# Splitting eight product groups among the last attention's score units

## What is computed

```
x = x + layernorm(attention(layernorm(x)))     # 16 heads of 64, causal, two null keys
x = x + layernorm(experts(layernorm(x)))       # four experts, the best two of a token weighted
# experts:
e0 = (silu(x @ sw_w1) * (x @ sw_w3)) @ sw_w2
e1 = gelu(sym @ me_c1w + b) @ me_c2w
e2 = h2 @ ce_gen_w
e3 = gelu(x @ ml_w1 + b) @ ml_w2
out = sum over the chosen e of weight_e * e
```

## Time and profile before

| | |
|---|---|
| median of three runs | 927.98 us (927.37 to 929.27) |
| span of the profiled execution | 927.0 us |
| PE busy | 867.1 us (94%) |
| DVE busy | 765.1 us (83%) |
| ACT busy | 585.8 us (63%) |
| POOL busy | 562.4 us (61%) |

### The profile page before, as it was taken

One profiled execution on the slowest core, in us unless ns is written; L12 is line 12 of the kernel. 1 busy time (PEld: TensorE's weight loads), 2 busy tenths in 40 slices (PEclk: granted clock), 3 DMA queues, 4 the chain that ended last, 5 costly groups with the idle time before them and its releaser, 6 DMA issues.

```text
span 927.0 us, 21283 instructions
## 1 busy us (share of the span) xinstructions
PE 867.1 (94%) x8062; PEld 689.6 (74%) x8062; DVE 765.1 (83%) x2457; ACT 585.8 (63%) x1255; POOL 562.4 (61%) x503
## 2 busy tenths in 40 slices
PE   0898899999999999999999999999999999999886
PEld 0685678688777878788787878678787878778676
DVE  6787799889898899889998899888998688865577
ACT  4518773967658672966648673866838774786631
POOL 5227763586638764586746865487644864467723
PEclk9989999999999999999999999999999999999999
DMA  6400000000000000000000000000000000000000
GB/s 165 113 1 0 13 2 2 1 12 2 14 1 0 13 2 13 1 13 1 14 1 1 13 2 14 0 13 2 2 13 1 1 13 2 1 1 1 3 12 12
DMA packets 21991, 11.46 MB, mean 12 GB/s; under 512 B 7552, under 2 KB 21248, under 8 KB 21760
## 3 DMA queue, kind: packets, MB, share of 16 engines
q1 hardware_dynamic: 20032, 9.50, 3.7%
q10 hardware_dynamic: 1856, 0.59, 0.3%
HBM read 7.99 MB, written 2.10 MB: 11 GB/s over the span
## 4 chain that ended last, share of the span: by engine, by line
PE 68%; DVE 16%; ACT 11%; issue 3%; POOL 1%; DMA 0%; SPq 0%; DVEq 0%; ACTq 0%; POOLq 0%
PE bank L1771 9%; PE bank L1772 8%; PE bank L1773 8%; PE bank L1784 5%; PE bank L2029 5%; PE bank L2086 4%; PE bank L1937 4%; PE bank L2035 3%; PE bank L2212 2%; PE bank L2218 2%; PE bank L2101 2%; PE bank L2076 2%; PE bank L2088 2%; PE bank L2187 2%; PE bank L2079 1%
## 5 line engine op out<-in xcount | busy, mean ns | idle before, releaser
L938 POOL TENSOR_TENSOR rnorm<-sumsq,minus_half 128x16 f32<-128x16 f32 x32 | 93.9, 2946 | 55.2 <-DVE sumsq L1574 55.2
L2029 PE MATMUL bank<-qT,kT 64*128 64x256 f32 x512 | 97.3, 387 | 0.0
L944 POOL TENSOR_TENSOR rnorm<-unit,minus_half 128x16 f32<-128x16 f32 x32 | 93.9, 2939 | 4.2 <-DVE unit L1580 4.2
L2035 PE MATMUL bank<-qT,kT 64*128 64x128 f32 x512 | 84.0, 284 | 5.1 <-ACT unit L1208 2.7
L1202 ACT ACTIVATE square<-bank,bias_k,rnorm 128x256 f32<-128x256 f32 x128 | 65.6, 570 | 35.8 <-PE bank L2029 35.8
L2035 PEld LDWEIGHTS bank<-qT,kT 64*128 64x128 f32 x512 | 71.0, 186 | 18.7 <-issue 5.7
L952 POOL TENSOR_SCALAR_AFFINE_SELECT square<-square 128x512 f32<-128x512 f32 x64 | 45.0, 704 | 61.6 <-ACT square L1208 61.5
L1132 ACT ACTIVATE xaT_hi<-bank 128x256 fp32r<-128x256 f32 x16 | 5.9, 382 | 111.1 <-PE bank L1945 110.7
L2029 PEld LDWEIGHTS bank<-qT,kT 64*128 64x128 f32 x512 | 68.7, 186 | 0.2
L2101 PE MATMUL bank<-w_out,qT 128*128 128x128 f32 x512 | 62.8, 276 | 1.2 <-DVE qT L1623 1.2
L1202 ACT ACTIVATE unit<-bank,bias_k,rnorm 128x256 f32<-128x256 f32 x96 | 51.4, 574 | 17.5 <-PE bank L2029 17.5
(11 more groups left out here) (419 smaller groups left out, 2902.7 us busy)
## 6 DMA issues: line engine op xcount, KB each, us to landing
xin<-in_L_attn_x SPq DMA_DIRECT2D x7, 256.0 KB, 2.8
out<-x SPq DMA_DIRECT2D x7, 256.0 KB, 2.3
square<-in_L_attn_w_kv SPq DMA_DIRECT2D x1, 1024.0 KB, 6.5
unit<-in_L_attn_w_q SPq DMA_DIRECT2D x1, 512.0 KB, 5.1
w_out<-in_L_attn_w_out SPq DMA_DIRECT2D x8, 64.0 KB, 2.1
xin<-in_L_attn_x ACTq DMA_DIRECT2D x1, 256.0 KB, 3.1
unit<-in_L_ffn_experts_gate ACTq DMA_DIRECT2D x1, 256.0 KB, 3.4
unit<-in_L_ffn_experts_up SPq DMA_DIRECT2D x1, 256.0 KB, 2.9
```

The costliest lines, as they stand in the source:

```text
L938: pool.tensor_tensor(rnorm[:, 1, t, :], sumsq[:, t % 2, :], minus_half[:], ALU.pow).then_inc(a_root.sem, 1)
L944: pool.tensor_tensor(rnorm[:, 0, ts, hs], k_sumsq[:, ts, hs], minus_half[:, hs].unsqueeze(1).to_broadcast([P, 2, H // 2]), ALU.pow).then_i ...
L2029: return mm(bank[s][:, 2 * P * i:2 * P * (i + 1)], kT[rs, p, 2 * P * b:2 * P * b + P], qT[rs, p, 2 * P * b:2 * P * (b + 1)], start=True, s ...
L2035: return mm(bank[2][:, 2 * P * s + P * i:2 * P * s + P * (i + 1)], kT[rs, p, ts], qT[rs, p, ts], start=True, stop=True)
```

## The change

The tables of PE and DVE for `LAST_A` are rewritten; those of ACT and POOL stay as they are. In the rest of the code, the operands of the last but one group's `f_out` go to buffers that attention does not use, and its results go in turn to banks 5 and 6. Each `f_out` can be asked for in two parts: part 0 is the products of `sw` and `me`, part 1 those of `gen` and `ml`.

```diff
@@ LAST_A
     "PE": """
-a_t.3 f_ce2T f_ml.3 a_v.2 a_v.3 f_out.0 a_scores.0 f_out.1 f_out.2 f_out.3 a_scores.1 a_nT a_mix.0 a_scores.2
-a_mix.1 a_scores.3 a_mix.2 a_scores.4 a_mix.3 a_scores.5 a_mix.4 a_scores.6 a_mix.5 a_scores.7 a_mix.6 a_out.0
-a_mix.7 a_out.1 F_turn.0 F_ce.0
+a_t.3 f_ce2T f_ml.3 a_v.2 a_v.3 a_scores.0 f_out.0.0 f_out.0.1 a_nT a_scores.1 a_mix.0 f_out.1.0 a_scores.2
+a_mix.1 f_out.1.1 a_scores.3 a_mix.2 f_out.2.0 a_scores.4 a_mix.3 f_out.2.1 a_scores.5 a_mix.4 f_out.3.0 a_scores.6
+a_mix.5 f_out.3.1 a_scores.7 a_mix.6 a_out.0 a_mix.7 a_out.1 F_turn.0 F_ce.0
     "DVE": """
-f_hid.1 a_ss.2 a_u.1 a_u.2 f_hid.2 a_ss.3 f_ce2 f_hid.3 f_ce2_apply a_u.3 f_pick a_nexp f_out.0 a_kss f_out.1
-f_out.2 f_out.3 a_nT a_mix.0 a_mix.1 f_end_stats a_mix.2 a_mix.3 a_mix.4 a_mix.5 a_mix.6 f_end a_o.0 a_mix.7 a_end.0
+f_hid.1 a_ss.2 a_u.1 a_u.2 f_hid.2 a_ss.3 f_ce2 f_hid.3 f_ce2_apply a_u.3 f_pick a_nexp a_kss f_out.0 a_nT
+a_mix.0 a_mix.1 f_out.1 a_mix.2 a_mix.3 f_out.2 a_mix.4 a_mix.5 f_out.3 a_mix.6 f_end_stats f_end a_o.0 a_mix.7 a_end.0
@@ buffers
+        hid_sw_late = [conv[:, 0, :], conv[:, 3, :], x1[:].rearrange("p t d -> p (t d)"), xn[:].rearrange("p t d -> p (t d)")]
+        hid_ml_late = [decay_row[:], *(unit_flat[:, i * N:(i + 1) * N] for i in (2, 3, 4))]
...
         def mix_bank(g, t):
+            if beside_ending(g):
+                return bank[5 + t % 2]
@@ POOL, late sum of units 0 and 1
-                    pool.wait_ge(f_e.sem, f_e.at(g - 1))
+                    if not ending(g):
+                        pool.wait_ge(f_e.sem, f_e.at(g - 1))
@@ ACT, f_ml
-                if j == 0 and not (known(g) and g == G - 1):
+                if j == 0 and g < G - 2:
                     act.wait_ge(a_ss.sem, a_ss.at(g + 1))
@@ PE, a_mix.0
+                elif ending(g):
+                    pe.wait_ge(f_meg.sem, f_meg.at(g - 1))
+                    pe.wait_ge(f_relu.sem, f_relu.at(g - 1))
                 else:
                     pe.wait_ge(f_eb.sem, f_eb.at(g - 1))
@@ PE, a_out.0
-                    if not ending(g):
+                    if ending(g):
+                        pe.wait_ge(f_eb.sem, f_eb.at(g - 1))
+                    else:
@@ PE, f_out
-            def f_out(g, t):
+            def f_out(g, t, part=None):
...
+                if beside_ending(g) and t > 1 and part != 1:
+                    pe.wait_ge(f_eb.sem, f_eb.at(g, E1 * (t - 1)))
```

More of the change, by code:

```diff
@@ L658, in ml_bank, with beside_ending, hid_sw_at, hid_ml_at @@
             return bank[2 + j % 2] if ending(g) else bank[4 + j % 2]
+        def beside_ending(g):
+            return g == G - 2
+        def hid_sw_at(g, j):
+            return (hid_sw_late if beside_ending(g) else hid_sw)[j]
+        def hid_ml_at(g, j):
+            return (hid_ml_late if beside_ending(g) else hid_ml)[j]
         def mix_bank(g, t):
+            if beside_ending(g):
+                return bank[5 + t % 2]
             return bank[(4, 5, 0, 1)[t]] if ending(g) else bank[4 + t]
@@ L1230, in f_ml_ @@
                 act.wait_ge(f_ml.sem, f_ml.at(g, j + 1))
-                if j == 0 and not (known(g) and g == G - 1):
+                if j == 0 and g < G - 2:
                     act.wait_ge(a_ss.sem, a_ss.at(g + 1))
-                act.activation(hid_ml[j], ml_bank(g, j)[:], ACT.Gelu, bias=b_ml[:, j:j + 1]).then_inc(f_mlg.sem, 1)
+                act.activation(hid_ml_at(g, j), ml_bank(g, j)[:], ACT.Gelu, bias=b_ml[:, j:j + 1]).then_inc(f_mlg.sem, 1)
             def f_ce_apply(g):
@@ L1710, in f_sw @@
                 gate, up = sw_banks(g, j)
-                V.scalar_tensor_tensor(out=hid_sw[j], in0=tanh_f(g, j), scalar=1.0, in1=gate[:], op0=ALU.add, op1=ALU.mult).then_inc(s.sem, 1)
+                hid = hid_sw_at(g, j)
+                V.scalar_tensor_tensor(out=hid, in0=tanh_f(g, j), scalar=1.0, in1=gate[:], op0=ALU.add, op1=ALU.mult).then_inc(s.sem, 1)
                 dve.wait_ge(s.sem, s.at(g, 2 * j + 1))
-                V.tensor_tensor(hid_sw[j], hid_sw[j], up[:], ALU.mult).then_inc(s.sem, 1)
+                V.tensor_tensor(hid, hid, up[:], ALU.mult).then_inc(s.sem, 1)
             def f_out(g, t):
@@ L2199, in f_ce2_apply @@
                 turn(bank[6], lambda t: ce_rows[:, t, :]).then_inc(f_gT.sem, 1)
-            def f_out(g, t):
+            def f_out(g, t, part=None):
                 ts = slice(t * P, (t + 1) * P)
-                if t == 0:
+                if t == 0 and part != 1:
                     pe.wait_ge(f_mlg.sem, f_mlg.at(g))
                     pe.wait_ge(f_meg.sem, f_meg.at(g))
-                    if ending(g):
+                    if ending(g) or beside_ending(g):
                         pe.wait_ge(f_hid.sem, f_hid.at(g))
-                    else:
+                    if not ending(g):
                         pe.wait_ge(f_cec.sem, f_cec.at(g))
+                if beside_ending(g) and t > 1 and part != 1:
+                    pe.wait_ge(f_eb.sem, f_eb.at(g, E1 * (t - 1)))
                 out_b = mix_bank(g, t)
[L2211 to L2214, removed]
+                if part != 1:
+                    for j in range(J1):
+                        mm(out_b[:, 0:P], hid_sw_at(g, j)[:, ts], w_sw2[:, j, :], start=(j == 0), stop=(j == J1 - 1))
+                    for j in range(2):
+                        mm(out_b[:, P:2 * P], hid_me[j][:, ts], w_c2[:, j, :], start=(j == 0), stop=(j == 1))
+                if part == 0:
+                    return
                 if not ending(g):
@@ L2217, in f_out @@
                 for j in range(J1):
-                    done = mm(out_b[:, 3 * P:], hid_ml[j][:, ts], w_ml2[:, j, :], start=(j == 0), stop=(j == J1 - 1))
+                    done = mm(out_b[:, 3 * P:], hid_ml_at(g, j)[:, ts], w_ml2[:, j, :], start=(j == 0), stop=(j == J1 - 1))
                 done.then_inc(f_e.sem, 1)
```

## The result

The changed kernel takes 936.15 us, the median of four runs (932.17 to 938.06), against 928.47 us for the kernel before, timed beside it: a ratio of 1.008, interval 1.006 to 1.010. Measured again with more runs, it took 934.46 against 928.36 us, a ratio of 1.0067 [1.0054, 1.0079]. With two more profiled executions there are twelve, with a median of 934.3, some 5.8 us over the kernel before; the first four alone are 7.7 us over it. The forecast was 931.8 (+3.8) with a range up to 934.0: the sign was right, the size was not.

What follows compares the result with a forecast made beforehand. It took the loop as bound by the PE-ACT ring (4.55 us a unit) and the end by one chain with 0.1 us slack on DVE. Loop −0.3, end +2.6, clock +1.5 gave +3.8: 931.8 us, range 929.6 to 934.0.

Steps and rivals of the forecast that it cites:

- The clock: PE's stop at the loop's start halves its clock for some 3 us of work: +1.5 us, ends 0 and 2.7.
- rival 2: A second clock fall at PE's stops ahead of `a_mix.7` and `a_out.1`: +1.5 us more, 933.3 us; chance 0.15.
- The end: On DVE, statistics behind `a_mix.6` and the wait for POOL's root delay the steps queued behind: +2.6 us.
- The loop: From unit 1 to `a_mix.6`: earlier start, less the added pieces and 0.2 us for hand-overs, net −0.3 us.
- Its first half: At the loop's start, unit 1 begins on PE at about 844.4, 1.3 us earlier.
- The pieces: Six `f_out` parts among the units, 7.4 us into some 5 us of waits: +0.8 us, ends 0 and +1.3.
- The turn: In a 4.55 us turn PE has 3.6 us taken, 0.94 free; pieces of 1.34 or 1.12 overrun by 0.4 or 0.2.
- The turn of 5.38 us: Unit 4's turn, with more exponentials on ACT: the added piece is free there.
- Rival 3: Not slower, the 2.6 us tail is hidden behind an earlier `a_mix.6`: about 926.4 us, or 927.9; chance 0.10.
- Rival 1: No clock fall at the loop's start: +2.3 us, 930.3 us; chance 0.15.
- Rival 4: Loop loses more: pieces +1.3, clock fall at its upper end 2.7; +5.5 us, 933.5 us or more; chance 0.13.

Runs made afterwards that it cites:

- warm_both: Changed kernel with unread products filling both PE stops: sixteen at the loop's start, ten ahead of `a_out.1`; 932.04 us, ratio 1.0042.
- stats_early: Changed kernel with the feed-forward statistics moved on DVE from behind to ahead of `a_mix.6`; 931.15 us, ratio 1.0025.
- warm_end: Changed kernel with only the stop at the loop's end filled, by ten unread products ahead of `a_out.1`; 933.37 us, ratio 1.0056.
- after_look2: Changed kernel, unaltered, in one more profiled execution; 934.06 us.
- before_late_stats: Kernel before with only `f_end_stats` moved on DVE from behind `a_mix.1` to behind `a_mix.6`; 933.0 us, ratio 1.0044.
- warm: Changed kernel with sixteen unread 128x512 products in PE's stop at the loop's start; 933.4 us, ratio 1.0047.
- warm_early: Changed kernel with sixteen unread products in the stop at the loop's start and the statistics ahead of `a_mix.6` on DVE; 929.36 us, ratio 1.0010.
- late_stats_warm: Kernel before with `f_end_stats` moved behind `a_mix.6` on DVE and ten unread products ahead of `a_out.1` on PE; 931.43 us, ratio 1.0038.
- four_ahead: Changed kernel's buffers and banks, with all four `f_out` groups ahead of the null transpose and the statistics where the kernel before has them; 929.51 us, ratio 1.0011.
- three_ahead: Changed kernel's buffers and banks, with three of four `f_out` groups ahead of the null transpose and the statistics early; 928.01 us, ratio 0.9995.
- after: Changed kernel, first profiled execution, the source of the profile shown; 932.17 us.
- after_again: Changed kernel, unaltered, timed again with more runs and a second profile; 934.46 us, ratio 1.0067.
- after_look1: Changed kernel, unaltered, in one more profiled execution; 934.26 us.

## Why the prediction was right in sign and too low

**The clock** is the step that failed: "I assume some 3 us of PE time at half ... I take **+1.5 us**", and with it the 0.15 given to rival 2. Against warm_both, whose stops are filled, `a_out.0` of the changed kernel's four profiled executions is 1.41, 1.61, 2.10 and 2.62 us later; stats_early and warm_end, whose stop is the same, lost 2.97 and 2.80. So the first fall costs 1.4 to 3.0 us: the value I took is its low end, and my upper end of 2.7 lies inside it. What was wrong in it is the 3 us at half clock, "one turn's worth": PE worked 3.1 to 6.4 us at half clock (table above). The trace of the kernel before has a fall that lasted 3.4 us (99.5 to 102.9, of which the earlier trace rows show the start), and falls of 6.8 us show only in the later executions.

The second fall adds 1.42 us (6.51 − 5.09 from `a_out.1` to routing) in one of four, near the 1.5 that rival 2 gave it. I argued against it with PE's 1.5 us of work between the two stops; after_look2 has that work and the fall, and before_late_stats, which has no stop at the loop's start, has it too.

The Trainium skill, page "TensorE: Matmul & The Clock Gate", section "The HAM clock gate", says that the throttled clock is the default state and that activity releases it. The runs agree in kind: filling a stop removed its fall in each profile (warm, warm_early and warm_both at the start; late_stats_warm, warm_both and warm_end at the end). Why the clock fell at the same stop of 2.31 us in some executions and not in others stays open. It also stays open what the two executions of 938 us held, since neither was profiled; their mean clock of 0.986, under the 0.988 of after_look2, says that they had more time at half clock than that one.

**The end** held: +2.6 forecast, 10.07 − 7.37 = 2.70 measured, with the 1.13 us wait for POOL's root in its place. POOL's masks of unit 7 waited behind that root as foreseen and cost nothing more. late_stats_warm measures the same term alone at 2.75.

**The loop** was mis-sized by half a microsecond, enough to turn its sign: −0.3 forecast, +0.25 measured (44.05 in warm_both against 43.80). Its first half was right: unit 1 comes 1.28 us earlier at full clock (10.58 against 11.86), as the forecast's 1.3. The pieces cost more than +0.8, outside even my upper end of +1.3. From unit 1 to unit 7 warm_both takes 29.83 us (40.41 − 10.58) and the kernel before 28.24, so 1.6 us. That upper end was added up wrongly: three overruns of 0.4 and two of 0.2 make 1.6.

The turn itself was also priced too low. From the late denominators to the next scores the forecast has 1.54 us, and with part 0 2.88; the profile above has 3.19 (856.49 to 859.68). The 0.31 us between them lie at two edges. Behind the last product of the values the next kind of product starts 0.33 us later (857.81 to 858.15), where the forecast counts 0.22; the trace of the kernel before has this too (748.15 to 748.49, in the stage ahead). And the piece takes 1.53 us up to the scores (858.15 to 859.68), one of part 1 1.31 (853.20 to 854.51), where I had taken 1.34 and 1.12 from products that followed each other. What the 0.19 us at a piece's edge is made of was not tried. The turn of 5.38 us went the other way: it takes 5.10 in warm_both, where the forecast left it as it was.

**Missed, without effect:** `scores.0` waits 0.69 us for ACT's copy of the values, which `f_out.0` used to cover. In the changed kernel PE waits for the null exponentials anyway, so it only shortened the stop, most of the way from the forecast's 5.7 us to 4.67; in four_ahead it counts.

So the profile above is 0.25 + 1.41 + 2.70 = 4.36 us, and after_look2 0.25 + 2.62 + 2.69 + 1.42 = 6.98. These are differences taken from one table and add up by construction; they size the terms. The 5.8 us between the medians lie between the two sums, 2.0 over the forecast. By difference, as an estimate, 0.55 of these are the loop, 0.1 the end and some 1.35 the clock.

Rival 3 fell: DVE ends `a_mix.6` later, not earlier, and nothing hides the tail. Rival 1 (no fall) is what warm_both shows, where the stops were filled by hand: +2.95 in the table, against its +2.3. Rival 4 had the loop's net size nearly right (+0.2) and put the clock at 2.7, which three of the six executions with this stop reach or come near (2.62, 2.80, 2.97).

## What to carry to other kernels

- When an edit makes TensorE stand still, price the clock's fall over its whole spread (here 1.4 to 3.0 us for one stop of 4.7 us), once for each stop, and not from one profiled execution. If the wait itself can't go, move real work of the engine into it, as three_ahead does with the same buffers. It is 6 us under the changed kernel, of which some 2.6 come from the place of the statistics.
- Small instructions put late into a queue whose end is the bound cost their length and their round trip to another engine (1.56 + 1.1 us here); one unit earlier, in stats_early, they cost 0.1 (7.49 us against 7.37 from `a_out.0` to `a_out.1`).
- Time a piece of work where it will stand, between other kinds of products: its edges, 0.3 us a turn here, count in each turn that the added work fills.

## What the runs showed of the hardware that was not expected

- The same stop, equal to 0.01 us, was followed or met by half clock for 3.4 us (after, after_again) and in other executions for 6.8 us (after_look1, after_look2, warm_end, stats_early), and what it cost was a little under half of the time that PE worked in it. A stop of 2.31 us ahead of `a_out.1` gave a fall in one of four executions of the changed kernel, and in the profiled ones of warm and before_late_stats.
- From start to start, half clock doubles a product: the null transpose takes 1.05 us to the next scores (842.86 to 843.91) against 0.53 in three_ahead (843.53 to 844.06). The sixteen products of `a_out.1` took 3.59 to 3.68 us in place of 2.05, less than double; the clock was back at 1.00 before their end (at 892.1, 891.6 and 891.4 in after_look2, warm and before_late_stats).
- Executions of one kernel reach the same place up to 2.2 us apart before the change's stretch is reached, which is as much as several terms of the sum. Counting from a fixed instruction removed it, and then the parts repeated to 0.1 us. The amount of half clock ahead of 830 us doesn't explain it: it was 10.2 us in thirteen of the fourteen profiles and 13.6 in that of four_ahead.
